# Routed experts on rows sorted by expert, between two halves of the second attention

## The reference, cut to what matters

```python
logits = xf @ router_w
topk_logits, topk_idx = jax.lax.top_k(logits, 2)
topk_w = jax.nn.softmax(topk_logits, axis=-1)
cw = jnp.zeros((T, E), xf.dtype).at[jnp.arange(T)[:, None], topk_idx].add(topk_w)
for e in range(E):
    h = xf @ w1[e] * jax.nn.silu(xf @ w_gate[e])     # 128 -> 256
    out = out + cw[:, e:e + 1] * (h @ w2[e])         # 256 -> 128
```

## Time and profile before

| | before |
|---|---|
| median of 3 runs | 3303.62 us |
| lowest, highest | 3297.83, 3314.3 us |
| profiled execution, span | 3294.6 us |
| PE busy | 2804.1 us (85%) |
| DVE busy | 2378.4 us (72%) |
| ACT busy | 1626.2 us (49%) |
| POOL busy | 1649.9 us (50%) |
| granted TensorE clock, mean | 0.947 |

### The profile page before, as it was taken

The page is one execution under the profiler, slowest core; times in us unless marked ns, Lnnn a source line. Parts: engine busy times, 40 slices in busy tenths (PEclk is TensorE's granted clock), DMA queues, the critical chain, the costliest instruction groups (busy, mean ns, idle before and its releaser), DMA issues. The chain is left out here.

```text
span 3294.6 us, 63646 instructions
## 1 busy us (share of the span) xinstructions
PE 2804.1 (85%) x20037; PEld 1750.0 (53%) x20037; DVE 2378.4 (72%) x5517; ACT 1626.2 (49%) x2647; POOL 1649.9 (50%) x1635
## 2 busy tenths in 40 slices
PE   0036489999999995999999999999999988999998
PEld 0024233333333334666666666666666656887877
DVE  8978548887888875666666666666666656888887
ACT  3444425554555552554454445445444535555554
POOL 4536512212212212555555555555555555888887
PEclk9987669999999996999999999999999998999999
DMA  2000022223223220111111110111011013223232
GB/s 51 0 7 0 10 88 98 77 78 102 75 79 102 74 59 20 35 32 36 36 33 30 37 37 27 37 36 33 31 37 37 27 58 114 92 89 96 82 99 64
DMA packets 174483, 177.37 MB, mean 54 GB/s; under 512 B 33840, under 2 KB 126065, under 8 KB 174322
## 3 DMA queue, kind: packets, MB, share of 16 engines
q1 hardware_dynamic: 174336, 175.47, 17.1%
HBM read 121.77 MB, written 43.12 MB: 50 GB/s over the span
## 5 line engine op out<-in xcount | busy, mean ns | idle before, releaser
L1705 DVE CUSTOM_DVE_ANT_0 a_scored<-a_pMax,a_causal 128x128 bf16<-128x128 f32 (+3 forms) x1024 | 450.0, 485 | 452.3 <-PE a_pMax L1873 452.3
L1010 DVE TENSOR_REDUCE a_max<-a_pair_banks 128x2 f32<-128x1024 f32 (+3 forms) x512 | 406.5, 821 | 167.4 <-PE a_pair_banks L624 97.1
L1618 ACT ACTIVATE a_PT<-a_pST 128x1024 f32<-128x1024 f32 (+1 forms) x384 | 339.0, 883 | 347.9 <-PE a_pST L1863 335.2
L1567 POOL TENSOR_SCALAR_AFFINE_SELECT a_PT<-a_PT 128x256 f32<-128x256 f32 x512 | 203.4, 410 | 600.5 <-ACT a_PT L1618 570.0
L944 ACT ACTIVATE a_PT<-a_pair_banks 128x1024 f32<-128x1024 f32 (+1 forms) x384 | 336.6, 883 | 333.7 <-PE a_pair_banks L624 192.3
L2130 POOL TENSOR_TENSOR m_silu<-m_silu,m_cw 128x512 f32<-128x512 f32 x256 | 400.5, 1589 | 130.0 <-ACT m_silu L2168 130.0
L2208 DVE TENSOR_TENSOR m_hT_low<-m_hT,m_hT_high 128x512 fp32r<-128x512 f32 x256 | 278.6, 1088 | 77.8 <-ACT m_hT_high L2155 77.7
L1881 PE MATMUL a_pO<-a_PT,a_V 128*64 128x512 f32 (+3 forms) x2048 | 303.9, 439 | 1.2 <-POOL a_PT L1567 1.2
L878 POOL TENSOR_TENSOR a_att<-a_att,a_rows 128x512 f32<-128x512 f32 x16 | 20.2, 1266 | 564.4 <-DVE a_att L1074 564.4
L2168 ACT ACTIVATE m_silu<-m_pG 128x512 f32<-128x512 f32 x256 | 153.0, 599 | 209.8 <-PE m_pG L2248 199.7
L1585 POOL TENSOR_TENSOR a_SM<-a_PT 128x768 f32<-128x768 f32 x128 | 235.0, 1836 | 10.6
(11 more groups left out here) (296 smaller groups left out, 7118.6 us busy)
## 6 DMA issues: line engine op xcount, KB each, us to landing
a_rden<-inverse_sums_dram SPq DMA_DIRECT2D x256, 128.0 KB, 2.8
m_cw<-cw_dram SPq DMA_DIRECT2D x32, 1024.0 KB, 5.5
a_KS<-k_parts_dram SPq DMA_DIRECT2D x64, 224.0 KB
a_QS<-q_parts_dram SPq DMA_DIRECT2D x64, 192.0 KB
a_xn_staged<-xn SPq DMA_DIRECT2D x32, 256.0 KB, 3.0
a_max_rows<-a_mT SPq DMA_DIRECT2D x512, 2.0 KB
q_parts_dram<-a_parts SPq DMA_DIRECT2D x16, 384.0 KB, 2.6
k_parts_dram<-a_parts SPq DMA_DIRECT2D x16, 384.0 KB
```

Of the source, the lines that this page charges most:

```text
L1010: last = v.tensor_reduce(MX[:, :, p, j], max_bank[m][:, :, at:at + (j + 1) * P], AX.X, ALU.max, negate=True)
L1567: g.affine_select(out=blocks, in_=blocks, compare_op=ALU.is_ge, fill=0.0, base=0, pattern=[[0, 2], [1, P]], channel_multiplier=-1).then_in ...
L1618: a.activation(PT[s.q % 2][:, :, k * TOK:k * TOK + w], pST[:, :, 0:w], ACT.Exp, scale=SCALE).then_inc(exped.sem, 1)
L1705: last = v.tensor_tensor_reduce(scored[:, cc, at:at + w], pMax[:, cc, at:at + w], causal[:, TOK - w:], -1.0, 3e38, ALU.add, ALU.min, MX[pa ...
```

## The change

Each token's row is computed by its two experts only.

- A new stage `route` runs before the attention. It turns all 16 sequences on PE, stores them as `xT_dram`, makes the logits, picks two experts for each token, and gives each of the 16384 (token, choice) pairs a slot in an order sorted by expert, in which each expert begins at a multiple of 256 rows. It leaves `slots`, the weights, and the expert of each of 71 tiles of 256 rows in SBUF.
- `attention1` is run twice, for sequences 0 to 7 and 8 to 15 (`part` 0 and 1). It no longer turns or routes; it loads `xT_dram` (`load_xT`). The split weights are made in part 0 and held.
- In part 0, POOL issues two indirect transfers at the end of each round (`dispatch`), each of which scatters a tile of 128 rows of `XN` to its slots in `xs_d`. For both halves' tokens that makes 128 in 64 rounds.
- `grouped` replaces `experts`: for each of 71 tiles, POOL loads the tile's expert into a register and copies this expert's split weights (1536 columns) into one of four buffers, PE turns the rows, makes the same three-matmul products on 256 columns, and turns the result back; SP stores it in `ys_d`.
- In part 1, POOL issues two indirect transfers at the end of each round (`gather`) that fetch the two results of 128 tokens; DVE weighs and adds them (`mix`, q = 1 and 5), ACT takes a tanh (`bend`, q = 2 and 6), DVE finishes the Silu and the output (`gate`, `finish`, q = 2 and 6), SP loads and stores the tokens (`load_xy`, `store_out`).
- `ffn` clears `xs_d` in memory: a memset on POOL, 18 transfers on SP behind its others.

```diff
+            for n in clears:
+                k = min(8, per - n)
+                sp.dma_start(into[:, n:n + k], zeros[:, 0:k * P].rearrange("p (n d) -> p n d", n=k)).then_inc(cleared, 16)
+            sp.wait_ge(cleared, 16 * len(clears))
...
-                    if s.next_x:
-                        qk_low.wait(pe, 2 * (r + 2) + 1)
-                        turn_x(b + 1)
...
-                    if s.next_x:
-                        qk_low.wait(pe, 2 * (r + 3) + 1)
-                        route(b + 1)
...
+                    if part == 0:
+                        dispatch(PB * b + q)
+                    elif q < TB:
+                        gather(0, b, 2 * NB - 1 if last else b, q)
+                    else:
+                        gather(1, b, b + NB - 1, q - TB)
+
+            def dispatch(n):
+                for choice in range(2):
+                    where = bass.IndirectOffsetOnAxis(ap=slots[:, choice, n:n + 1], axis=0)
+                    g.indirect_dma_start(xs_d, where, XN[:, n, :], None).then_inc(scattered, 16)
+
+            def gather(h, b, j, t):
+                finished[h].wait(g, b - 1)
+                for choice in range(2):
+                    n = TB * j + t
+                    where = bass.IndirectOffsetOnAxis(ap=slots[:, choice, n:n + 1], axis=0)
+                    g.indirect_dma_start(G[h][choice][:, t * P:(t + 1) * P], None, ys_d, where).then_inc(gathered[h], 16)
...
+            def bend(h, b):
+                mixed[h].wait(a, b)
+                a.activation(G[h][1], G[h][0], ACT.Tanh, scale=0.5).then_inc(bent[h].sem, 1)
...
+                    if part == 1 and q == 2 and not first:
+                        bend(1, b - 1)
+                    if part == 1 and q == 6:
+                        bend(0, b)
...
+            def mix(step, h, b, j):
+                v.wait_ge(gathered[h], 16 * 2 * TB * (b + 1))
+                for n in range(2):
+                    part_of = G[h][n].rearrange("p (t d) -> p t d", t=TB)
+                    step.did(v.tensor_tensor(part_of, part_of, over(weight[:, n, bass.ds(j * TB, TB)], P), ALU.mult))
+                step.wait()
+                v.tensor_tensor(G[h][0], G[h][0], G[h][1], ALU.add).then_inc(mixed[h].sem, 1)
+
+            def gate(step, h, b):
+                bent[h].wait(v, b)
+                v.scalar_tensor_tensor(G[h][1], G[h][1], 1.0, G[h][0], ALU.add, ALU.mult).then_inc(gated[h].sem, 1)
+                gated[h].wait(v, b)
+
+            def finish(step, h, b, y, loaded):
+                v.wait_ge(xy_loaded[h], loaded)
+                step.then(v.scalar_tensor_tensor(G[h][1], G[h][1], 0.5, y, ALU.mult, ALU.mult))
+                v.tensor_tensor(Ys[h], G[h][1], Xs[h], ALU.add).then_inc(finished[h].sem, 1)
...
+                    if part == 1:
+                        if q == 1 and not first:
+                            mix(step, 1, b - 1, b + NB - 2)
+                        if q == 2 and not first:
+                            gate(step, 1, b - 1)
+                            finish(step, 1, b - 1, Ys[1], 32 * b)
+                        if q == 5:
+                            mix(step, 0, b, 2 * NB - 1 if last else b)
+                        if q == 6:
+                            gate(step, 0, b)
+                            if not last:
+                                finish(step, 0, b, Ys[0], 32 * (b + 1))
...
+            for i in range(NTL):
+                e = g.value_load(tile_expert[0:1, i:i + 1], min_val=0, max_val=E - 1)
+                added.wait(g, i - WDEEP)
+                src = W[:, bass.ds(e, 1)].rearrange("p o n h -> p (o n h)")
+                g.tensor_copy(WS[i % WDEEP][:].rearrange("p n h -> p (n h)"), src).then_inc(w_here.sem, 1)
...
+            for i in range(NTL + 3):
+                if some(i - 1):
+                    high(i - 1)
+                if some(i + 1):
+                    split_x(i + 1)
+                if some(i):
+                    silu(i)
+                if some(i - LAG):
+                    yT_evac(i - LAG)
+                if some(i - 3):
+                    y_evac(i - 3)
...
+            for i in range(NTL + 1):
+                if some(i - 1):
+                    rest_h(i - 1)
+                if some(i + 1):
+                    rest_x(i + 1)
+                if some(i):
+                    make_h(i)
...
+            route(nc, NB, XN, ident, router_w, xT_d, slots, weight, tile_expert)
...
+            attend(0)
+            grouped(nc, given, weights_in, w2, xs_d, ys_d, tile_expert, ident)
+            attend(1)
```

More of the change, by code:

```diff
@@ L1379, in attention1 @@
+def attention1(nc, part, FIRST, NB, XN, ident, held, w_o, x1_d, y_d, xT_d, xs_d, ys_d, rden_d, w1, w_gate, given, w_in, slots, weight, out):
     HEADS, DH = 16, 64
@@ L1825, in _ @@
             invert(NG - 1)
-            weights()
+            if part == 1:
+                mix(tail[0], 1, NB - 1, 2 * NB - 2)
             o_over_sums(NG - 1, GB - 1)
+            if part == 1:
+                gate(tail[0], 1, NB - 1)
+                finish(tail[0], 1, NB - 1, Ys[1], 32 * NB)
             y_sum(NG - 1, GB - 1, NB - 1)
+            if part == 1:
+                y_added.wait(v, NG - 1)
+                finish(tail[0], 0, NB - 1, Y[:], 32 * NB - 16)
         @block.tensor
         def _(pe):
-            def turn_x(b):
-                pe.wait_ge(staged, 16 * b + 16)
-                for t in range(TB):
-                    mm = pe.transpose(pM[1][:, t * P:(t + 1) * P], xst[:, t * P:(t + 1) * P], ident[:])
-                mm.then_inc(x_turned.sem, 1)
             def project(pair, n):
@@ L1912, in values @@
                 mm.then_inc(v_ready.sem, 1)
-            def route(b):
-                for t in range(TB):
-                    mm = pe.matmul(pM[1][:, t * E:(t + 1) * E], XT[:, t * P:(t + 1) * P], wr[:], start=True, stop=True)
-                mm.then_inc(l_ready.sem, 1)
-            for n in range(6):
+            for n in range(6 if part == 0 else 0):
                 if n >= 2:
@@ L2065, in at @@
-        def at(b, e, back):
-            n = E * b + e - back
-            return n, (e - back) % E, not (isinstance(n, int) and n < 0)
+        W2 = sb("w2_given", [P, E, H])
+        W = sb("w_parts", [P, E, 6, H], F32R)
+        WS = [sb(f"w_tile{i}", [P, 6, H], F32R) for i in range(WDEEP)]
+        X = [sb(f"x{i}", [P, J, P]) for i in range(DEEP)]
+        XH, XL = ([sb(f"xT_{n}{i}", [P, ROWS], F32R) for i in range(2)] for n in ("high", "low"))
+        SG, HT = ([sb(f"{n}{i}", [P, HC, ROWS]) for i in range(2)] for n in ("silu", "hT"))
@@ L2179, in _, with split_x @@
-            turns(a, NB, turn)
-            high(NB * E - 1, E - 1)
-            acc_silu(NB - 1)
+            for n in range(3):
+                if n == 2:
+                    a.wait_ge(w2_in, 16)
+                for half in range(2):
+                    es = slice(half * E // 2, (half + 1) * E // 2)
+                    a.copy(W[:, es, 2 * n], raw[n][:, es]).then_inc(w_high, 1)
+            def split_x(i):
+                x_turned.wait(a, i)
+                u_ready.wait(a, i - 2)
+                a.copy(XH[i % 2][:], pX[i % 2][:, 0:ROWS]).then_inc(x_high.sem, 1)
@@ L2229, in _, with rest_x @@
-            turns(v, NB, turn)
-            for k in range(HC):
-                low(NB * E - 1, E - 1, k)
-            yT_evac(NB - 1)
+            for n in range(3):
+                for half in range(2):
+                    v.wait_ge(w_high, 2 * n + half + 1)
+                    es = slice(half * E // 2, (half + 1) * E // 2)
+                    v.tensor_tensor(W[:, es, 2 * n + 1], raw[n][:, es], W[:, es, 2 * n].bitcast(F32), ALU.subtract).then_inc(w_low, 1)
+            def rest_x(i):
+                x_high.wait(v, i)
+                v.tensor_tensor(XL[i % 2][:], pX[i % 2][:, 0:ROWS], XH[i % 2][:].bitcast(F32), ALU.subtract).then_inc(x_low.sem, 1)
```

675 lines of the change are left out of this document (338 added, 337 removed).

## The result

| | before | after |
|---|---|---|
| median | 3308.49 us | 3144.36 us |
| lowest, highest | 3297.83, 3314.3 us | 3138.57, 3156.32 us |
| profiled execution, span | 3294.6 us | 3140.4 us |
| granted TensorE clock, mean | 0.947 | 0.923 |

A forecast was written before the change was run, and what follows sets the result against it. Experts were taken as PE-bound, attention1's odd rounds as set by a serial DVE-SP chain, even ones by PE. Terms -341 + 57 + 14 + 15 + 46 + 10 = -199 on 3294.6, plus 9.0 outside: 3105 us, range 3035 to 3240.

The forecast's parts named there:

- Experts out, grouped in: Last stage: 566 us of experts go, 71 tiles at 2.85 us plus ends come, 225 us; net -341 us.
- two bounds: Grouped stage, POOL's register load: 0 us if all beside the copy, 1.6 us behind a copy of 2.4; taken as hidden.
- rival (C): Longer grouped tile: POOL's load and copy in series, 4 us, 3187; or PE at 1.2 GHz, 4.7 us, 3236; 0.16 together.
- Route: New stage before attention: 33 us of turning and routing on PE, 20 of sorting on DVE, 4 for boundaries; +57 us.
- Two halves: Attention run twice: two bodies, starts of 34 and 30, tails of 80 together; 1491 us against 1477, +14 us.
- 1395 - 27, all of it real: Attention body: without turning and routing, 15 x 1.77 = 27 us go, leaving 1368 over 126 rounds, 10.86 each.
- D = 1.3: POOL's rounds: one indirect transfer costs 1.3 us; two fit for nothing in the idle 4.84 us while D is under 2.42.
- rival (D): POOL's indirect transfers bound the attention rounds: 3249 us at D = 3 (0.04), 3497 at D = 4 (0.11); chance 0.15.
- 15 us allowed for crossing small transfers: Attention rounds of both parts: indirect transfers cross the small transfers of the maxima, +15 us (0 to 40).
- Mix, gate, finish: Part 1 on DVE: mix hidden; gate and finish push the serial chain's head by 3.3 us, 14 times, +46 us.
- Rival (B): Part 1: gate and finish cost nothing as the chain has more slack, 3059 us; chance 0.10.
- The clears: Clearing xs_d during ffn: 9.3 MB in 18 transfers taking 150 us, hidden; without this cover 50 to 150 us.

The follow-up runs named there:

- copy_small: All_three with POOL copying 128 instead of 1536 columns of an expert's weights for each tile behind the fourth: 3044.32 us, grouped stage 194.1 us against 193.6.
- low_x_later: The kernel after, with DVE's split of the next sequence (low_x) moved behind the first maxima and the inversion of round q = 5: 3129.55 us.
- scatter_none: All_three without part 0's indirect transfers, so no row is scattered and the experts work on zeros: 3037.05 us.
- rows_first: The kernel after, with SP issuing the four maxima rows first in each round, ahead of the inverses and the sums: 3033.06 us.
- rows_first_three: All_three with SP also issuing the maxima rows first in each round: 2962.35 us, ratio 0.8942 to before.
- All_three: The kernel after, with gate and finish one round later, sorted rows loaded four tiles ahead, and low_x behind the first maxima: 3036.50 us.
- scatter_four: All_three with four indirect transfers instead of two in each of part 0's rounds: 3099.33 us, part 0 +55.5 us.

## Why the prediction was right, and where it was off

**Experts out, grouped in.** The mechanism holds, and 244 us stand where 566 stood. The term was 19 us short, all in the tile, 3.13 for 2.85. Two steps of it failed and partly cancelled. SP's stream was not read as a queue: the loads stand behind stores that wait for outputs, +0.55 us a tile. And the compute was priced too high: 2.58 us is PE's own pace, where I had 2.7 for PE and let a loop of DVE and ACT make it 2.85 by adding durations end to end; copy_small shows that this loop has slack. POOL's copy, 1.47 us, is hidden, as taken. The register load is 0.29 us with 0.15 behind it, on POOL's sequencer, and lies beside the copy before: at 2202.39 it begins, and that copy runs from 2202.41 to 2203.88. Of the forecast's two bounds this is the lower, and with a clock of 1.00 in the stage rival (C) falls in both its forms.

**Route.** 62 us for 57. The sort is right. The step that failed is "both turned buffers alternate and PE is busy most of the time", from which I took nearly warm products: PE was busy all the time and stayed at 1.2 GHz, 16 x 2.45 = 39 us for the 33.

**Two halves.** "1395 - 27, all of it real" failed. Of the turned sequence's 1.78 us a block of eight rounds, only the 1.03 of the even round went. In the odd round the chain through `low_x` took its place: before, this round was 11.74 us, now it is 12.05, where another odd one is 11.15. low_x_later takes the round to 11.15 and gives 11 us back in part 0. The forecast took an observed round as a bound without asking which engine set it. Each body has this round seven times, at about 1.1 us over the 11.0 that the forecast gives it: 7 to 8 us of the 11 that part 0's body is over, and half of part 1's 14. The starts hold, 35 and 29 us for 34 and 30, and part 0's tail too. Part 1's tail is 43 us for 50: the last block's mix, gate, finish and store cost some 3 us there, not 10.

**The indirect transfers.** D = 1.3 was taken from SP's rows and is 1.27 us, and rival (D) doesn't come about. The 15 us allowed for crossing small transfers are some 8 in part 0 (scatter_none), though the crossing itself isn't shown; part 1's odd rounds are 0.25 to 0.3 us longer again, some 8 us, which no run took apart. The Trainium skill, GPSIMD Engine Reference, section "Performance pitfalls for Q7 kernels", would have made D 10.9 us by its cost of one gather index; 128 indices in 0.97 us show that it doesn't speak of these transfers. The Trainium skill, SBUF — State Buffer, section "SBUF: two separate sides", says that a DMA issued from GpSimd waits for its descriptors while a DVE operation holds the port they share. The trace agrees in sign: the 15 transfers that begin beside the first two operations of `mix` (L1934) take 1.26 us each, the 38 of part 1 beside an idle DVE 0.96 in the mean.

```profile
2710.39 1.26 POOL L1773 DMA_INDIRECT m_w<-y_sorted_dram,slots  x1 [0.15 <-issue]
```

**Mix, gate, finish.** Place and sign hold: mix is hidden (in low_x_later both kinds of even rounds behind it are at 10.77), gate and finish cost 42.5 us for 46, and part 1's body is 49 us longer than part 0's, for the 46 of the forecast. That the size fits is partly luck. The forecast had 14 x 3.3 us, all through SP's rows; the two push the head by 2.6 us and lengthen the 14 rounds by 33 us in all, through PE's next maxima as well as through the rows, and 10 us come from the low clock in the even rounds behind, which the forecast didn't have. Rival (B), no cost, falls.

**The clears** are hidden: SP issues the 18 transfers from 194.1 to 213.8 us, the last has landed at 218.7, and PE's first matmul behind `ffn` is at 389.5 us for 389.2 before. They take 25 us and not the 150 of the forecast, which put their rate too low.

**The bill.** Grouped +19, route +5, starts 0, tails -6, part 0's body +11, part 1's body +14, the stages ahead +1, outside the span -5 (4.0 for 9.0): 39 us. The last is no cost of the kernel: the forecast took a median less the span of one execution, and each execution after the change that has both on record is 1.8 us over its own span. That the total came within 1.3% owes something to errors of both signs.

## What to carry to other kernels

Read a queue engine's stream as a program: SP's queue cost 40 us in one stage and 74 to 111 in the attention, and each time a transfer that was ready stood behind one that waited. Before a round's length is used as a price, find what sets it and what its floor would be; work taken from a round held by something else gives back less than it cost, and work put ahead of a serial chain costs most of its length (2.3 us a round for 2.6 here). Price a pipelined loop by its busiest engine first, and by a chain of durations only where the trace shows the wait.

## What the runs showed of the hardware

A wait can cost more than its length. PE waits 1.66 us until 2710.50, and from about 2711.7 it runs for 3.4 us at the 1.2 GHz level (windows of the kernel after; the two left out are at 0.50 too):

```profile
2708.00:2711.00 3.00, 1.34 (x12) 0.86 (x12) 2.89 (x4) 0.00 (x0) 2.77 (x3) 1.00 0.18 58
2711.00:2712.00 1.00, 1.00 (x7) 0.31 (x7) 1.00 (x4) 0.96 (x2) 0.69 (x2) 0.83 1.00 301
2712.00:2713.00 1.00, 1.00 (x5) 0.25 (x3) 0.95 (x6) 0.19 (x2) 0.98 (x2) 0.50 0.69 201
...
2715.00:2716.00 1.00, 1.00 (x14) 0.30 (x10) 0.00 (x0) 0.46 (x1) 0.00 (x0) 0.96 0.00 0
```

```profile
2711.43 4.07 PE L2059 MATMUL a_pO<-a_PT,a_V 128*64 128x512 f32 x16
```

The same products take 2.38 us otherwise. 11 of the 61 in part 1's body were over 3.5 us, 3 of 61 in part 0's, none of 125 before, none of 61 in part 1 of rows_first, where 15 waits of up to 1.4 us for the maxima are left, and none of 61 in part 1 of rows_first_three; a wait of 1.63 us at 2687.66 was not followed by a slow one, so it doesn't happen each time. The other way round, PE ran through the route stage without a gap at 0.50.

128 rows of 512 bytes are sent off by one indirect transfer in 0.97 us of POOL's time. Once in part 0, between its 113th and 114th transfer, POOL stands for 3.1 us:

```profile
1993.36 0.98 POOL L1766 DMA_INDIRECT x_sorted_dram<-xn,slots  x1 [3.14 <-issue]
```

All_three and rows_first_three have the same stop at the same transfer, and scatter_four has it there and at the 227th, 4.0 and 3.9 us long, which are its two rounds of over 18 us. What it is, no run shows.
